# Layer norm, spin attention and a mixture of experts on one core: who normalises, splits and routes, and at which step

## The reference

```python
s = einsum('bni,oi->bno', xn, W_spin) + b_spin            # the spins
g = einsum('bmd,od->bmo', mean(s, axis=1), W_global)
e = einsum('bnd,od->bno', s, W_J)
A = softmax(einsum('bnd,bmd->bnm', e, s) / sqrt(128))     # 2048 x 2048 for each batch
attn = tanh(beta * (s + g + A @ s))

logits = xn @ Wg.T + bg                                   # 16 experts, top 2, softmax of the two
gate, up = (xn @ Wgu[e] + bgu[e]) split in even and odd columns
gated = (clip(up, -7, 7) + 1) * min(gate, 7) * sigmoid(1.702 * min(gate, 7))
ffn = sum over the two experts of weight * (gated @ Wd[e] + bd[e])
out = x + attn + ffn
```

## Time and profile before

| what | value |
|---|---|
| median of 3 runs | 475.68 us (472.8 to 479.76) |
| the profiled execution's own time | 475.99 us |
| its span (first to last instruction) | 474.3 us |
| around the span | 1.7 us |
| busy: PE, DVE, ACT, POOL | 357.0, 304.2, 259.4, 212.3 us |
| mean granted TensorE clock | 0.883 of full speed |

### The profile page before, as it was taken

The page is one execution under the profiler, slowest core; times in us unless marked ns, Lnnn a source line. Parts: engine busy times, 40 slices in busy tenths (PEclk is TensorE's granted clock), DMA queues, the critical chain, the costliest instruction groups (busy, mean ns, idle before and its releaser), DMA issues.

```text
span 474.3 us, 5954 instructions
## 1 busy us (share of the span) xinstructions
PE 357.0 (75%) x1772; PEld 288.0 (61%) x1774; DVE 304.2 (64%) x599; ACT 259.4 (55%) x517; POOL 212.3 (45%) x247
## 2 busy tenths in 40 slices
PE   2878998895316953189999798999986578779492
PEld 1656886573305741068888698888865466567271
DVE  4979689992105820069797687878775078767266
ACT  5857666563006521066878386777873165447361
POOL 4437942267763777400000334334327645727530
PEclk9979999998566985569999999999999669989976
DMA  6996000001110111100020166666453314425421
GB/s 188 348 338 234 1 0 1 23 28 50 55 53 0 61 50 50 39 1 30 1 67 22 46 193 188 183 201 193 156 152 105 101 59 113 116 68 138 105 68 45
DMA packets 41414, 45.92 MB, mean 97 GB/s; under 512 B 3828, under 2 KB 33140, under 8 KB 41388
## 3 DMA queue, kind: packets, MB, share of 16 engines
q1 hardware_dynamic: 36220, 32.94, 22.2%
q0 software_dynamic: 5168, 12.67, 9.4%
HBM read 23.46 MB, written 22.12 MB: 96 GB/s over the span
## 4 chain that ended last, share of the span: by engine, by line
PE 44%; DVE 23%; another core or an unknown queue 12%; issue 11%; ACT 6%; DMA 2%; POOL 1%; SPq 1%; ACTq 0%; DVEq 0%; POOLq 0%
PE PS L496 12%; PE PS L498 11%; PE PS L497 10%; DVE mx L1009 6%; DVE pl L994 5%; PE PS L550 5%; DVE pl L1156 1%; ACT ph L861 1%; PE PS L652 1%; PE PS L719 1%; PE PS L706 1%; ACT xn L786 1%; DMA xy<-slots_x 1%; DVE sl L1035 1%
## 5 line engine op out<-in xcount | busy, mean ns | idle before, releaser
L852 ACT ACTIVATE PS<-PS 128x512 f32<-128x512 f32 x128 | 74.8, 585 | 144.5 <-PE PS L498 71.0
L994 DVE TENSOR_TENSOR pl<-PS,ph 128x512 fp32r<-128x512 f32 x128 | 87.7, 686 | 66.7 <-ACT ph L861 44.2
L1009 DVE TENSOR_REDUCE mx<-PS 128x1 f32<-128x512 f32 x128 | 84.6, 683 | 58.3 <-remote 35.4
L550 PE MATMUL PS<-xT,gq 128*128 128x512 f32 x128 | 52.7, 450 | 42.8 <-DVE mx L1009 27.5
L861 ACT ACTIVATE ph<-PS 128x512 fp32r<-128x512 f32 x128 | 76.5, 598 | 12.1 <-ACT PS L852 0.4
L496 PE MATMUL PS<-ph,rows 128*128 128x512 f32 x128 | 56.1, 439 | 31.0 <-DVE pl L994 27.9
L457 POOL DMA_INDIRECT slots_x<-xn,posu x64 | 61.9, 968 | 19.8 <-issue 18.9
L496 PE MATMUL PS<-gq,xT 128*128 128x512 f32 x128 | 56.3, 440 | 6.0 <-issue 4.9
L550 PEld LDWEIGHTS PS<-xT,gq 128*128 128x128 f32 x128 | 25.7, 203 | 56.4 <-DVE mx L1009 35.4
L497 PE MATMUL PS<-pl,rows 128*128 128x512 f32 x128 | 53.6, 419 | 0.0
L498 PE MATMUL PS<-ph,rows 128*128 128x512 f32 x128 | 53.4, 417 | 0.0
(11 more groups left out here) (187 smaller groups left out, 714.3 us busy)
## 6 DMA issues: line engine op xcount, KB each, us to landing
slots_y<-yr SPq DMA_DIRECT2D x20, 512.0 KB, 3.1
slots_x<-xs SPq DMA_DIRECT2D x1, 5120.0 KB, 21.8
xy<-slots_x SPq DMA_DIRECT2D x20, 256.0 KB, 3.0
xn<-in_L_attn_x SPq DMA_DIRECT2D x8, 256.0 KB, 4.1
w_f<-in_L_ffn_Wgu SPq DMA_DIRECT2D x1, 2048.0 KB, 12.4
late<-in_L_ffn_Wgu SPq DMA_DIRECT2D x1, 2048.0 KB, 18.0
xs<-in_L_attn_x SPq DMA_DIRECT2D x8, 256.0 KB, 3.2
out_y<-made SPq DMA_DIRECT2D x7, 256.0 KB, 2.8
```

The lines of the kernel that those rows point to most:

```text
L550: mm(o, gq[:, k % 3, 0, a * P:(a + 1) * P], xT[k // CB][:, 0, 512 * c:512 * c + 512], start=True, stop=True).then_inc(mx_fill, 1)
L852: A(S[:, n % 3], S[:, n % 3], ACT.Exp).then_inc(exp_done, 1)
L994: v.tensor_tensor(dst, S[:, n % 3], high.bitcast(F32), ALU.subtract).then_inc(s_lo, 1)
L1009: v.tensor_reduce(mx4[:, a, c:c + 1], MX[:, n % 2], AX.X, ALU.max).then_inc(mx_free, 1)
```

## The change

- **Head.** Chunks 0, 1 and 3 are normalised by VectorE (`tensor_scalar`), chunk 2 by ScalarE. Chunks 4 and 5 are normalised by ScalarE in halves, chunks 6 and 7 by VectorE at steps 0 and 1 (`scalar_tensor_tensor`). For chunks 4 to 7 GpSimd computes scale and shift (`scales`, with a power of -0.5), instead of ScalarE's root and VectorE's reciprocal. `moments(6)`, `moments(7)` and `queries_lo(1)` stand behind `shifts(0)`. The Hh/Hl product is earlier, the exponential's table is loaded earlier.
- **GpSimd's order.** It waits for all four chunks of the first batch before it writes `rows[0]`, has `scales(4)` to `scales(7)` among and behind them, and waits for chunk 7 to be normalised before it folds the weights. The eight operations L414 and L416 go: ScalarE copies one expert's high part at each second step from 26 to 56, VectorE subtracts two experts at each of steps 44 to 47 and 60 to 63.
- **Spins.** Odd pairs go to the second half of bank pair `O`, so two are in flight. In the second batch: one pair at step 1, two at steps 2 to 4, one at step 5. The turns of chunks 4 to 7 stand at the end of steps 0 to 3.
- **Routing** starts at step 6 and ends at 22. Two small operations go to GpSimd, a 128x512 copy to ScalarE, the tile count is made by three small operations instead of a 128x512 comparison and sum. The mean's broadcast goes to ScalarE.
- **rows[1].** ScalarE writes the high part at steps 24 to 27, VectorE the low part at steps 28 to 31, so nothing of it stands between GpSimd's two bursts any more.

Semaphore declarations, the waits that count them and a few lines that only follow from these are left out of the diff. Lines are dedented.

```diff
@@ -192,9 +195,15 @@
-SPIN_AT = {2 + h: (1, h) for h in range(8)}
-GLOBAL_AT = {11: 0, 13: 1}
-COUNT_AT = {17: 0, 19: 1}
+SPIN_AT = {1 + n: [(1, h) for h in hs] for n, hs in enumerate(((0,), (1, 2), (3, 4), (5, 6), (7,)))}
+GLOBAL_AT = {8: 0, 10: 1}
+COUNT_AT = {13: 0, 15: 1}
+ROW_HI_AT = {24 + c: c for c in range(CB)}
+ROW_LO_AT = {28 + c: c for c in range(CB)}
+WEIGHT_HI_AT = {26 + 2 * n: n for n in range(NE)}
+WEIGHT_LO_AT = {(44, 60)[n // 8] + n % 8 // 2: (n // 2 * 2, n // 2 * 2 + 1) for n in range(NE)}
 def field_at(i):
@@ -213,8 +222,8 @@
-    if i in SPIN_AT:
-        e_order.append(("S", *SPIN_AT[i]))
+    for use in SPIN_AT.get(i, ()):
+        e_order.append(("S", *use))
@@ -224,6 +233,16 @@
+def e_at(use):
+    return O[:, 1] if use[0] == "S" and use[2] % 2 else E
+def e_before(use):
+    n = e_no[use]
+    odd = [use[0] == "S" and use[2] % 2 for use in e_order[:n + 1]]
+    return max([m + 1 for m in range(n) if odd[m] == odd[n]], default=0)
 def mx_no(k, q):
@@ -389,12 +409,33 @@
-    for c in range(CB):
-        pool.wait_ge(xn_ready[0], c + 1)
+    def rows_of(c):
...
+    def scales(c):
+        n, q = c - CB, slice(4 * c, 4 * c + 4)
+        pool.wait_ge(dev_in, c + 1)
+        g.tensor_scalar(mv[:, q, 1], mv[:, q, 1], EPS, None, ALU.add).then_inc(var_up, 1)
+        g.tensor_scalar(mv[:, q, 0], mv[:, q, 0], -1.0, None, ALU.mult).then_inc(var_up, 1)
+        pool.wait_ge(var_up, 2 * n + 2)
+        g.tensor_tensor(rstd[:, q], mv[:, q, 1], nhalf[:], ALU.pow).then_inc(root, 1)
+        pool.wait_ge(root, n + 1)
+        g.tensor_tensor(shift[:, q], mv[:, q, 0], rstd[:, q], ALU.mult).then_inc(scale_ready, 1)
+    for c in range(CB):
+        pool.wait_ge(xn_ready[c], 1)
+    pool.wait_ge(consts, 14)
+    rows_of(0)
+    rows_of(1)
+    scales(4)
+    rows_of(2)
+    rows_of(3)
+    for c in range(5, NCH):
+        scales(c)
+    pool.wait_ge(xn_ready[NCH - 1], 1)
@@ -408,20 +449,17 @@
-    pool.wait_ge(w_row, 16)
-    for k in range(4):
-        q = slice(k * NE // 4, (k + 1) * NE // 4)
-        g.tensor_copy(wh[:, q], w_f[:, q]).then_inc(w_hi, 1)
-        pool.wait_ge(w_hi, k + 1)
-        g.tensor_tensor(wl[:, q], w_f[:, q], wh[:, q].bitcast(F32), ALU.subtract).then_inc(w_lo, 1)
...
+    pool.wait_ge(exp_dlt, 1)
+    g.tensor_scalar(mk[:, 7], mk[:, 5], 1.0, None, ALU.add).then_inc(share, 1)
...
+    pool.wait_ge(share, 2)
+    g.tensor_tensor(w12[:, 1], w12[:, 0], mk[:, 5], ALU.mult).then_inc(share, 1)
@@ -442,15 +480,11 @@
-            for k in range(CB, NCH):
-                t = 4 * (k - CB)
-                pool.wait_ge(row_h[1], k - CB + 1)
-                g.tensor_tensor(rows[1][:, 1, t:t + 4, 1:D], xn[:, TB + t:TB + t + 4, 1:D],
-                                rows[1][:, 0, t:t + 4, 1:D].bitcast(F32), ALU.subtract)
...
-            g.memset(rows[1][:, 1, :, 0:1].bitcast(F32), 0.0).then_inc(row_l[1], 1)
+            g.memset(rows[1][:, 1, :, 0:1].bitcast(F32), 0.0).then_inc(row_c, 1)
...
+        pool.wait_ge(share, 3)
@@ -504,10 +538,9 @@
     def e_bank(*use):
-        n = e_no[use]
-        if n:
-            pe.wait_ge(e_free, n)
-        return E
+        if e_before(use):
+            pe.wait_ge(e_free, e_before(use))
+        return e_at(use)
     def mx_bank(k, q):
@@ -560,20 +593,20 @@
     def idle_products(n):
...
-            mm(O[:, 1], Hh[:], xT[0][:, 0, 0:512], start=True, stop=True)
+            mm(O[:, 1, P:2 * P], ident[:], ident[:], start=True, stop=True)
...
-    turn_tokens(1)
...
+    turn_tokens(1)
+    pe.wait_ge(h_cut, 1)
+    idle_products(3)
...
-    pe.wait_ge(h_cut, 1)
+    idle_products(3)
...
-    idle_products(4)
...
-    idle_products(6)
     def spins_and_logits(b, h):
@@ -656,8 +689,6 @@
-        if i in TURN_AT:
-            turn_tokens(TURN_AT[i])
@@ -671,8 +702,10 @@
-        if i in SPIN_AT:
-            spins_and_logits(*SPIN_AT[i])
+        for use in SPIN_AT.get(i, ()):
+            spins_and_logits(*use)
+        if i in TURN_AT:
+            turn_tokens(TURN_AT[i])
@@ -780,11 +813,15 @@
-    def normalise(c):
-        act.wait_ge(rstd_ready, c + 1)
-        for t in range(4 * c, 4 * c + 4):
+    def normalise(c, first=0, last=4):
+        if c < CB:
+            act.wait_ge(rstd_ready, c + 1)
+        else:
+            act.wait_ge(scale_ready, c - CB + 1)
+        for t in range(4 * c + first, 4 * c + last):
...
-        ins.then_inc(xn_ready[c // CB], 1)
+        if last == 4:
+            ins.then_inc(xn_ready[c], 1)
     def tokens_hi(c):
@@ -800,50 +837,45 @@
     def spins_out(b, h):
...
-        A(sl[:, t:t + 2], E[:, 0:2 * AC].rearrange("p (a n) -> p a n", a=2), ACT.Copy).then_inc(e_free, 1)
+        A(sl[:, t:t + 2], e_at(("S", b, h))[:, 0:2 * AC].rearrange("p (a n) -> p a n", a=2), ACT.Copy).then_inc(e_free, 1)
...
-    normalise(0)
-    deviation(1)
...
-    normalise(1)
+    deviation(1)
+    tokens_hi(0)
...
-    tokens_hi(0)
+    act.wait_ge(h_fill, 1)
+    A(Hh[:], O[:, 1, P:2 * P], ACT.Copy)
+    A(Cg[:], O[:, 1, 2 * P:3 * P], ACT.Copy, scale=1.0 / N).then_inc(h_out, 1)
...
-    act.wait_ge(h_fill, 1)
-    A(Hh[:], O[:, 1, P:2 * P], ACT.Copy)
-    A(Cg[:], O[:, 1, 2 * P:3 * P], ACT.Copy).then_inc(h_out, 1)
...
-    normalise(3)
-    A(brow[:], O[0:1, 0, 0:P], ACT.Copy)
-    A(AE[:, 0, 0:D], O[:, 0, 0:D], ACT.Copy)
-    A(AE[:, 1, 0:D], O[:, 0, 0:D], ACT.Copy)
...
-    deviation(4)
-    deviation(5)
...
+    act.wait_ge(w_cut, 1)
+    A(brow[:], O[0:1, 0, 0:P], ACT.Copy)
+    A(AE[:, 0, 0:D], O[:, 0, 0:D], ACT.Copy)
+    A(AE[:, 1, 0:D], O[:, 0, 0:D], ACT.Copy).then_inc(w_out, 1)
+    A(warm[:], epsc[:], ACT.Exp)
...
-    normalise(4)
-    deviation(6)
-    deviation(7)
-    A(warm[:], epsc[:], ACT.Exp)
...
+    normalise(4, 0, 2)
...
-    normalise(5)
+    normalise(4, 2, 4)
...
-    normalise(6)
+    normalise(5, 0, 2)
...
+    normalise(5, 2, 4)
     def exponent(i):
@@ -875,6 +907,12 @@
+    def mean_out(b):
+        act.wait_ge(mean_in, b + 1)
+        if b:
+            act.wait_ge(e_fill, e_no["M", b - 1] + 1)
+        A(mean_bc[:], ident[:], ACT.Identity, bias=xsum[:, b, CB:CB + 1], scale=0.0).then_inc(mean_ready, 1)
     def squash(k):
@@ -886,14 +924,14 @@
-        if i in TURN_AT:
-            tokens_hi(TURN_AT[i])
...
-        if i in SPIN_AT:
-            spins_out(*SPIN_AT[i])
+        for use in SPIN_AT.get(i, ()):
+            spins_out(*use)
+        if i in TURN_AT:
+            tokens_hi(TURN_AT[i])
@@ -901,17 +939,28 @@
-        if i == 14:
+        if i in (7, 9):
+            mean_out(i // 2 - 3)
+        if i == 13:
+            act.wait_ge(e_fill, e_no["R", 0] + 1)
+            act.wait_ge(route_dve, 3)
+            A(bufs[3].rearrange("p (e t) -> p e t", e=NE), E.rearrange("p (t e) -> p e t", t=NT),
+              ACT.Copy).then_inc(e_free, 1)
+        if i == 10:
...
-        if 34 <= i < 38:
-            if i == 34:
+        if i in WEIGHT_HI_AT:
+            n = WEIGHT_HI_AT[i]
+            if n == 0:
+                act.wait_ge(w_row, 16)
+            A(wh[:, n], w_f[:, n], ACT.Copy).then_inc(w_hi, 1)
+        if i in ROW_HI_AT:
+            c = ROW_HI_AT[i]
+            if c == 0:
...
-            c = i - 34
...
-    normalise(7)
@@ -988,6 +1037,18 @@
+    def normalise(c):
+        if c < CB:
+            dve.wait_ge(rstd_ready, c + 1)
+            for t in range(4 * c, 4 * c + 4):
+                ins = v.tensor_scalar(xn[:, t, 1:D], xn[:, t, 1:D], rstd[:, t:t + 1], shift[:, t:t + 1], ALU.mult, ALU.add)
+        else:
+            dve.wait_ge(scale_ready, c - CB + 1)
+            for t in range(4 * c, 4 * c + 4):
+                ins = v.scalar_tensor_tensor(out=xn[:, t, 1:D], in0=xn[:, t, 1:D], scalar=rstd[:, t:t + 1],
+                                             in1=shift[:, t:t + 1].broadcast_to([P, D - 1]), op0=ALU.mult, op1=ALU.add)
+        ins.then_inc(xn_ready[c], 1)
     def lo(use, dst, high):
@@ -1015,9 +1076,7 @@
     def mean_step(b):
...
-        link(v.tensor_reduce(xsum[:, b, CB:CB + 1], xsum[:, b, 0:CB], AX.X, ALU.add))
-        link(v.tensor_scalar(xsum[:, b, CB:CB + 1], xsum[:, b, CB:CB + 1], 1.0 / N, None, ALU.mult))
-        v.tensor_scalar(mean_bc[:], ident[:], 0.0, xsum[:, b, CB:CB + 1], ALU.mult, ALU.add).then_inc(mean_ready, 1)
+        v.tensor_reduce(xsum[:, b, CB:CB + 1], xsum[:, b, 0:CB], AX.X, ALU.add).then_inc(mean_in, 1)
     def global_in(b):
@@ -1040,42 +1099,39 @@
+    normalise(0)
...
+    moments(2)
...
-    moments(2)
+    normalise(1)
...
+    dve.wait_ge(h_out, 1)
+    v.tensor_tensor(Hl[:], O[:, 1, P:2 * P], Hh[:].bitcast(F32), ALU.subtract).then_inc(h_cut, 1)
...
-    dve.wait_ge(h_out, 1)
-    v.tensor_tensor(Hl[:], O[:, 1, P:2 * P], Hh[:].bitcast(F32), ALU.subtract).then_inc(h_cut, 1)
+    normalise(3)
...
-    moments(4)
-    moments(5)
...
-    inverse(4)
-    inverse(5)
-    for a in range(4):
-        maximum(0, a, a, 0)
+    for q in range(4):
+        maximum(0, q, q, 0)
+    moments(4)
...
+    for q in range(4, 8):
+        maximum(0, q, q % 4, q // 4)
```

(57 more changed lines are left out.)

22 lines of the change are left out of this document (13 added, 9 removed).

## The result

The changed kernel takes 485.82 us (median of 4 runs, 484.75 to 487.89) where the kernel before takes 474.24 (median of 4): a ratio of 1.027, with a 95% interval of 1.019 to 1.035. It is 2.7% slower. Forecast were 472 us, and a range up to 480.

What follows compares the result with a forecast made beforehand. Limits were taken by stretch: VectorE in head and routing, TensorE in steps 0 to 9 and behind the bursts, late TensorE signals in the scatter bursts. Terms -6.1 + 0.2 + 1.5 + 0.5 = -3.9 gave 472 us, range 458 to 480.

Steps and rivals of the forecast that it cites:

- Head, -6.1: Up to the exponent of step 0: maxima start 2.0 us earlier, VectorE needs 13.7 us instead of 17.9; 6.1 us saved.
- Steps 0 to 5, 16.1: Step 0 plus five steps with the eight spin pairs, bounded by TensorE: 16.1 us, with 1 us counted for delayed `prob_lo(0)`.
- Steps 6 to 20, 31.5 and 0.7 for legs over GpSimd: VectorE bounds these steps with low parts, maxima and routing: 31.5 us, plus 0.7 for routing's legs over GpSimd.
- Rival 4: Steps 1 to 6: GpSimd's weight fold or constants hold VectorE operations, costing up to 2.3 us; 474 us, chance 0.08.
- Burst length, 83.0: GpSimd's two scatter bursts become one: 41.6 us, a pause of 0.9 and 40.5, together 83.0 us.
- Steps that pass in the second half, 3: Second half of the merged scatter burst: it starts disturbed and 3 steps pass, bounds 0 and 7.
- 1.3 us from the last DMA until the first exponent: End of the merged scatter burst: the first exponent behind it, step 31, starts 1.3 us after the last DMA.
- coming out of a burst costs extra: Steps just behind the scatter bursts: 2.9 us more than at 1.77 us a step, at a lower clock.
- Rival 2: Second half of the merged burst: no step passes and it ends slower, +6.7 us for the stretch; 477 us, chance 0.13.
- Rival 1: Merged burst: the short pause is enough and 7 steps pass in the second half, -5.6 us; 465 us, chance 0.27.
- Rival 3: Head: it doesn't get shorter, as spin copies or turns, not VectorE, set its rhythm; 478 us, chance 0.10.
- the weights' 0.5: rows[1] and weight splitting moved to ScalarE and VectorE: +0.5 us, bounds 0 to +4.

Runs made afterwards that it cites:

- rows_back: The changed kernel with the low-part subtractions of rows[1] back on GpSimd between its two scatter bursts, not on VectorE: 472.96 us, ratio 1.002 to the kernel before.
- pause_only: The changed kernel with a bare GpSimd wait for the exponent of step 31 between its scatter bursts, subtractions staying on VectorE: 476.49 us, ratio 1.006 to the kernel before.
- head_fix: The changed kernel with two spin pairs in each of steps 2 to 5 and chunks 6 and 7 normalised by ScalarE: 479.95 us, ratio 1.012 to the kernel before.
- nopause: The kernel before with only the low-part subtractions of rows[1] moved from GpSimd to VectorE at steps 44 to 47: 482.81 us, ratio 1.022 to the kernel before.
- pace4: The changed kernel with its 64 scatter DMAs in groups of four, each held until an exponent 3.5 steps later: 417.50 us, ratio 0.881 to the kernel before.

## Why the prediction was wrong

- **Head, -6.1: right in kind, -4.7 measured.** Between the first maxima and the exponent of step 0 it took 16.7 us, forecast 16.8. The term mis-sized is the start of the maxima: 18.90, only 0.5 us earlier than before and not 2.0. Input times differ between executions, and nine profiled executions with this head have exponent 0 at 34.7 to 38.4, mean 36.0.
- **Steps 0 to 5, 16.1: failed, 22.5 measured.** The step that failed is "TensorE can be two scores ahead, so I count 1 us". I priced the delay for `prob_lo(0)` and not for the low part of chunk 4 in the same queue, which step 1's spins need. This costs 3.0 us of wait and about 1.5 of low clock. Both halves of the cause are shown: moving the spins brought 2.1 us, moving the normalisations 2.4 more. The first figure rests on one profiled execution (20.4 us, against 22.2 to 23.6 in nine with the old head), the second on four (18.0 to 18.5). Of the 1.9 us between 18.0 and the forecast 16.1, 0.5 are TensorE's own work, priced too low (16.6 us busy at full clock), and the rest are waits.
- **Steps 6 to 20, 31.5 and 0.7 for legs over GpSimd: right** (31.9). Rival 4 didn't come: no operation of VectorE beside the fold took over 0.69 us. All of them read PSUM, which the cast doesn't, so the rival had nothing to catch. Nor does every operation of GpSimd hold that cast: in the changed kernel it took 0.21 us inside a GpSimd power operation of 1.04 us (L424).
- **Burst length, 83.0: right** (82.6), and so was the pause (0.6 for 0.9).
- **Steps that pass in the second half, 3: nearly** (2). "First exponent behind is 31" was 30; that is 1.8 us. The rows were counted a little off, without harm: 6 exponents start in the first burst (27 to 32; 26 starts just ahead of it), 7 in the pause, 6 in the second.
- **1.3 us from the last DMA until the first exponent: failed, 8.9 measured.** This is the other step that failed. I took the first exponent behind a burst of 32 for the end of the delay. It is not: in the kernel before, exponents 34 and 47 start at 146.26 and 201.74 after 2.3 us of waiting each, 5.2 and 4.9 us behind the last DMA, and 17.0 and 25.8 us behind their products. (The reading of 131.8 to 142.68 had the wrong product, too: that one is of step 35, and step 33's ended at 115.20, so its signal was 27 us late.) The last late exponent comes 3.7 to 5.2 us behind rows of 32 or 33 DMAs (`before`, `rows_back`, `pause_only`), and 8.2 to 9.0 behind 65 (changed kernel twice, `head_fix`, `nopause`). Part of this stood in the forecast as "coming out of a burst costs extra", 2.9 us, which did not show as such. So the delay behind the burst was priced at 4.2 us in all, and is 8.9. In sum 7.6 + 1.8 - 2.9 - 1.1 (small differences) = 5.4 us over the 172.4 forecast.
- **The rivals.** Rival 2 has the stretch right (177.6 for 177.8), but not the way: two steps passed, and the lost time is the delay behind the burst. Rival 1 is refuted: a single pause of 0.6 us is not enough behind 33 DMAs. It said 7 steps. Rival 3 is refuted: the head became 4.7 us shorter.
- **Sum.** -4.7 + 6.3 + 6.9 (instead of -6.1 + 0.2 + 2.0, the weights' 0.5 included), and 3.3 behind step 79, which varies by itself: +11.8 us of span. The chance of 0.07 for slower was too small: it asked that rivals 2 and 3 meet, and left out that a loss in the burst and one in the first steps can meet instead.

Most of all, the prediction treated the bursts as a landscape to lay steps over, 83 us that are lost in any case. It moved the six steps of the pause elsewhere and booked the 14.4 us as saved, though its own reading, "about 7 steps pass in each burst, mostly in its first third", says that the DMAs behind a pause are free for a while.

## What to carry to other kernels

Where one engine's waits end in no event of the profile beside a long row of indirect DMAs, spread these DMAs over the steps by waiting on the progress of the main loop: where the kernel before takes 473 to 477 us it took 9 to 13% off, and no other edit moved more than 3%; on the fourth chip it gained nothing. So time the kernel before on more than one chip. Before a pause of a queue is filled or closed, ask what drains in it. And when work moves onto an engine ahead of a loop, price the delay for every consumer in its queue, not just for the first.

## What the runs showed of the hardware

- **TensorE's signals are late beside long rows of indirect DMAs.** DMAs at one in 1.27 us without a pause don't disturb the signals sent beside the first six or seven of them. Then signals come late and in the order in which they were sent, up to 45 us after the product (`nopause`: 47). ScalarE's and VectorE's signals arrive within 0.1 us beside the same DMAs. The delay reaches beyond the row: the last late exponent comes 3.7 to 5.2 us behind 32 or 33 DMAs, 8.2 to 9.0 behind 65.
- **What counts is not the number of DMAs.** At one in 1.6 us on average, in rows of at most 8 with pauses of 0.5 to 4.5 us, the same 64 delay a waiting exponent by 3.8 us at most. Rows of 8 or 9 with seven pauses lie between (5.9 us). That this is a queue which drains in the pauses fits all runs; which part of the chip holds it no run shows. The data are not the likely cause: the DMA engines are 14% busy in the standing part of the burst, and 49% busy in the window of the fourth chip, where no signal is late.
- **It depends on the chip, or on its state.** On three chips the kernel before took 473 to 477 us, on a fourth 384, with GpSimd's DMAs within 6% of the same rate (one gather in 1.32 to 1.35 us there, in 1.28 to 1.32 elsewhere). On that one pacing gains nothing. Each chip was seen in one group of runs. What sets them apart is open.
- **TensorE's clock follows.** In the standing part of the burst the granted clock is 0.55, that is mostly 1.2 GHz, with TensorE idle for up to 16 us at a time; in `pace4` it is 1.00 throughout the same DMAs, with TensorE busy 93%.
